# A rank count over a sparse adjacency: the last quarter of the rows moves from TensorE's recurrence to VectorE's scans

## The chip, the cores and the metric

One core of a Trainium2 chip runs the whole program. The metric is the device time of one execution in microseconds; three runs of the kernel before gave a median of 110.85 us (110.51 to 111.42).

## The reference, cut to what matters

The input is x (2048 x 64, f32) and a 0/1 adjacency adj (2048 x 2048, f32, about two ones in a row). Two graph layers follow each other, each with a residual and a layer norm:

```
support = x @ weight
rank = cumsum(adj != 0, axis=1); deg = rank[:, -1:]; k = min(deg, 100)
pos = rank - (deg - k)
w = mask * where(pos > 0, 0.5 ** (k - pos), 0)          # 2048 x 2048
x = layernorm(x + w @ support + bias)
deg = clip(sum(adj, 1) + 1, 1)
h = (adj @ x + x) / deg
z = concat([x, h]) @ W + b
x = layernorm(x + relu(z) / max(norm(relu(z)), 1e-12))
```

So in layer 0 every nonzero of a row gets a weight of one half to the power of the number of nonzeros to its right (beyond 100 it is zero). Layer 1 multiplies by the adjacency itself.

## The kernel before, in words

The rows are taken in four quarters q of 512, each as four tiles of 128 rows. The columns are taken in 16 blocks b of 128, from the right.

SyncE loads adj in 16 units of 1 MB (a quarter's 512 rows by 512 columns) into the ring `stage` of eight places; a place is loaded again when TensorE has transposed what lay there (lines 232 to 246). TensorE transposes two blocks of a unit at a time, 8 matmuls into one of two PSUM banks `tmp` (`transpose_adj`, line 834), and VectorE copies the bank to `adjT` (line 545). The last four of the 16 units, (2,1), (3,1), (2,0) and (3,0), go another way: VectorE casts them to `nat` (`pack`, line 497) and SyncE issues four DMA transposes (line 249).

The count is a recurrence in PSUM. `count` (line 856) adds block b with the triangular matrix `suffix` and block b+1 with `rest` to a bank `cnt` of 128 columns by 512 rows. ScalarE turns the bank into bf16 weights by a Relu that writes int16 (`weights`, line 326; the exponent bits are the count). The next `count` of the same bank waits until ScalarE has read it. `weigh` (line 870) multiplies the weights by `sup`, the support in three bf16 parts, in four matmuls of 192 columns, three steps behind. Two banks (c = 0 and 1) run next to each other: bank 0 takes quarter 0 and then quarter 2, bank 1 takes quarter 1 and then quarter 3, 16 steps each.

The order is written out by hand. TensorE's loop (line 970) runs over ticks: count of bank 0, weigh of bank 0, the transposition two ticks ahead (`fill`), count of bank 1, weigh of bank 1. VectorE and ScalarE have loops over the same marks (lines 506 and 348). Between the copies VectorE finishes quarters 0 and 1 (`finish_layer0`, line 458): part 0 sums the three parts out of PSUM, 1 adds x, 2 and 3 measure and centre, 4 is the inverse root and x1, 6 and 7 split y = x1 @ W for layer 1. `WHEN` says at which mark after a quarter's end each part stands, `X1T_AT` at which mark TensorE transposes x1.

After the ticks TensorE aggregates layer 1: `aggregate(g, blocks, tiles)` (line 903) is a row of 194-column matmuls from `adjT` and `ysp`. The parts that need only quarters 0 and 1 of y (`early`) cover VectorE's finish of quarters 2 and 3. GpSimd adds the identity to the diagonal blocks of `adjT` (line 285) before the aggregation reads them. VectorE, ScalarE and GpSimd then finish the output in five batches.

## Time and profile before

| | |
|---|---|
| median of three runs | 110.85 us |
| the profiled execution, its own time | 110.75 us |
| its span, first to last instruction | 108.8 us |
| TensorE matmul busy | 92.6 us, 85% |
| VectorE busy | 63.4 us, 58% |
| ScalarE busy | 57.4 us, 53% |
| GpSimd busy | 18.8 us, 17% |
| granted TensorE clock, mean | 0.974 |

The profiled execution took 1.95 us more than its span. Busy time is an average over stages; the stages here are the ticks (to about 75 us), the aggregation (to about 99 us) and VectorE's tail. Matmul durations are modelled and overlap; the distance between the starts of two matmuls says what one costs.

### The profile page before, as it was taken

The page shows a single profiled execution, that of the slowest core. Times are in us where ns is not written, and L with a number is a line of the kernel's source. Part 1 is how long each engine was busy: PE and PEld are TensorE (multiplying, and loading weights), DVE is VectorE, ACT ScalarE, POOL GpSimd, SP SyncE. Part 2 cuts the span into 40 slices and gives each one's busy share as a digit, 9 for nine tenths or more (in the row PEclk, how much of TensorE's full clock was granted, in tenths as well). Part 3 has the DMA queues.
Part 4 walks back from the last instruction along what each step waited for, and adds up shares of the span by engine and source line. Part 5 has one row for each costly group of instructions (what it writes and reads, how often), then busy time and mean ns, then how long its engine had stood idle before and what let it go on. Part 6 is the DMA issues. An engine that isn't in the chain of part 4 may idle for free.

```text
span 108.8 us, 2398 instructions
## 1 busy us (share of the span) xinstructions
PE 92.6 (85%) x886; PEld 72.4 (67%) x886; DVE 63.4 (58%) x188; ACT 57.4 (53%) x125; POOL 18.8 (17%) x44
## 2 busy tenths in 40 slices
PE   5938789999999999999996799999999999995000
PEld 2326448677778777776764477779989999994000
DVE  2224632352862424389799934148983339999991
ACT  0503866453766565756577486783032208478740
POOL 6200000000000009000009500000000000467860
PEclk9999999999999999999999999999999999999955
DMA  2999999999979999996979970000000000000124
GB/s 52 315 339 358 349 321 350 385 387 389 383 234 399 388 387 386 386 386 236 193 141 121 202 136 0 6 0 0 0 6 0 0 0 6 0 0 12 36 54 94
DMA packets 23867, 20.23 MB, mean 186 GB/s; under 512 B 13617, under 2 KB 17713, under 8 KB 23857
## 3 DMA queue, kind: packets, MB, share of 16 engines
q1 hardware_dynamic: 23696, 20.06, 60.4%
q8 instruction: 7, 0.11, 0.4%
q10 hardware_dynamic: 160, 0.03, 0.1%
q14 instruction: 4, 0.02, 0.1%
HBM read 17.47 MB, written 0.52 MB: 165 GB/s over the span
## 4 chain that ended last, share of the span: by engine, by line
PE 65%; DVE 17%; DMA 11%; issue 3%; ACT 1%; ACTq 1%; DVEq 0%
PE acc L878 17%; PE cnt L865 10%; PE cnt L867 10%; PE tmp L846 9%; PE acc L909 7%; DMA adjT<-nat 6%; DMA wd<-in_L_gnn_weight_dram 5%; PE cnt L909 5%; PE tmp L897 3%; DVE stats L447 3%; DVE t L582 3%; DVE adjT L545 2%; DVE t L593 1%; PE acc L923 1%; PE tmp L923 1%
## 5 line engine op out<-in xcount | busy, mean ns | idle before, releaser
L330 ACT ACTIVATE wts<-cnt 128x512 int16<-128x512 f32 x64 | 37.8, 596 | 20.4 <-PE cnt L867 20.1
L878 PEld LDWEIGHTS acc<-sup,wts 128*128 128x128 bf16 x256 | 22.8, 98 | 13.7 <-issue 0.5
L878 PE MATMUL acc<-sup,wts 128*128 128x192 bf16 x256 | 30.8, 246 | 0.0
L545 DVE COPY adjT<-tmp 128x1024 bf16<-128x1024 bf16 x24 | 16.4, 688 | 20.3 <-PE tmp L846 20.3
L865 PE MATMUL cnt<-adjT,rest 128*128 128x512 bf16 x60 | 22.7, 379 | 3.7 <-DMA adjT<-nat 1.6
L867 PE MATMUL cnt<-adjT,suffix 128*128 128x512 bf16 x64 | 24.2, 379 | 0.0
L285 POOL TENSOR_TENSOR adjT<-adjT,ident 128x128 bf16<-128x128 bf16 x16 | 7.3, 492 | 50.4 <-PE cnt L867 50.4
L846 PE MATMUL tmp<-ident,stage 128*128 128x128 bf16 x192 | 14.5, 219 | 0.7 <-DMA stage<-in_adj_dram 0.7
L846 PEld LDWEIGHTS tmp<-ident,stage 128*128 128x128 bf16 x192 | 12.3, 98 | 1.8 <-issue 1.2
L909 PE MATMUL acc<-ysp,adjT 128*128 128x194 bf16 x128 | 11.8, 247 | 0.0
L909 PEld LDWEIGHTS acc<-ysp,adjT 128*128 128x128 bf16 x128 | 10.8, 98 | 0.3
L289 POOL TENSOR_TENSOR small<-square,power 128x4 f32<-128x4 f32 (+1 forms) x4 | 4.2, 1053 | 33.4 <-DVE square L614 33.4
L865 PEld LDWEIGHTS cnt<-adjT,rest 128*128 128x128 bf16 x60 | 5.9, 98 | 5.6 <-ACT wts L330 3.0
L383 ACT ACTIVATE u<-u,degree 128x64 f32<-128x64 f32 x16 | 4.4, 336 | 4.8 <-DVE degree L578 4.7
L497 DVE CAST nat<-stage 128x512 bf16<-128x512 f32 x16 | 6.7, 467 | 0.1
L867 PEld LDWEIGHTS cnt<-adjT,suffix 128*128 128x128 bf16 x64 | 6.3, 98 | 0.3
L909 PE MATMUL cnt<-ysp,adjT 128*128 128x194 bf16 x64 | 6.0, 247 | 0.0
L447 DVE BATCH_NORM_STATS2 stats<-t 128x6 f32<-128x128 f32 x23 | 5.7, 285 | 0.1
L483 DVE TENSOR_TENSOR left<-tmp,ysp 128x256 f32<-128x256 f32 x4 | 1.7, 424 | 6.5 <-ACT ysp L341 6.5
L909 PE MATMUL tmp<-ysp,adjT 128*128 128x194 bf16 x64 | 5.5, 247 | 0.0
L909 PEld LDWEIGHTS cnt<-ysp,adjT 128*128 128x128 bf16 x64 | 5.4, 98 | 0.0
L909 PEld LDWEIGHTS tmp<-ysp,adjT 128*128 128x128 bf16 x64 | 5.3, 98 | 0.0
(101 smaller groups left out, 85.3 us busy)
## 6 DMA issues: line engine op xcount, KB each, us to landing
stage<-in_adj_dram SPq DMA_DIRECT2D x12, 1024.0 KB, 13.3
stage<-in_adj_dram SPq DMA_DIRECT2D x8, 512.0 KB, 8.0
xs<-in_x_dram SPq DMA_DIRECT2D x2, 256.0 KB, 6.0
out_dram<-xs SPq DMA_DIRECT2D x3, 128.0 KB, 2.0
out_dram<-xs SPq DMA_DIRECT2D x2, 64.0 KB, 1.7
wd<-in_L_gnn_W_dram SPq DMA_DIRECT2D x4, 16.0 KB, 7.9
adjT<-nat SPq DMA_TRANSPOSE x4, 5.0
wd<-in_L_gnn_weight_dram ACTq DMA_DIRECT2D x2, 16.0 KB, 4.8
```

Of the source, the lines that this page charges most:

```text
L285: nc.gpsimd.tensor_tensor(d, d, ident16[:, :], ALU.add).then_inc(diag_ready, 1)
L289: nc.gpsimd.tensor_tensor(small[:, 3, batch(k)], square[:, batch(k)], power[:, 0:size(k)], ALU.pow).then_inc(norm_ready[k], 1)
L330: nc.scalar.activation(wts[:, c, n % WRING, :].bitcast(I16), cnt[:, c, :], ACT.Relu).then_inc(w_ready[c], 1)
L383: nc.scalar.activation(u1[:, t, :], u1[:, t, :], ACT.Copy, scale=degree[:, t:t + 1]).then_inc(weighted[k], 1)
L447: yield nc.vector.bn_stats(stats[:, k, t:t + 2, :].rearrange("p s c -> p (s c)"), data[:, t:t + 2, :].rearrange("p t d -> p d t"))
L497: nc.vector.tensor_copy(nat[:, i, r, :], stage[:, u % RING, r, :]).then_inc(nat_ready, 1)
L545: nc.vector.tensor_copy(adjT[:, q, bp // 2, :, bp % 2 * 2:bp % 2 * 2 + 2, :], bank.bitcast(BF16).rearrange("p (r k n) -> p r k n", r=RT, k ...
L846: last = nc.tensor.transpose(bank[:, (2 * r + k) * P:(2 * r + k + 1) * P], halves[:, r, 2 * j0 + 1:2 * (j0 + P):2], ident16[:, :])
L865: nc.tensor.matmul(cnt[:, c, :], rest[:, :], block_of(q, b + 1), start=False, stop=False, skip_group_check=True)
L867: nc.tensor.matmul(cnt[:, c, :], suffix[:, :], block_of(q, b), start=(b == NB - 1), stop=True, skip_group_check=True).then_inc(cnt_done[c], 1)
L878: last = nc.tensor.matmul(acc[:, c * RT + r, 0:PD], wts[:, c, n % WRING, r * P:(r + 1) * P], sup[:, b, :], start=(b == NB - 1 and r % 2 == ...
L909: last = nc.tensor.matmul(agg[g][:, r, 0:PD + 2], adjT[:, g, b // QB, r, b % QB, :], ysp[:, b, 0:PD + 2], start=first, stop=(b == NB - 1), ...
```

## The change

Quarter 3 leaves the recurrence. Its rows are loaded as four tiles of 128 whole rows (1 MB each, the same ring). VectorE runs `tensor_tensor_scan` over each tile from the right, 512 columns at a time, 16 scans in all, at marks 11 to 27; each writes int16 ranks into the low halves of the f32 words it read. GpSimd turns the words into bf16 (`bare`, 16 times 128x512), SyncE transposes each tile by DMA (`turn`, 128x2048), ScalarE makes weights (`mix`, 16 times 128x512) and GpSimd makes 0/1 of the transposed tile again (`bare_adj`, four times 128x2048). TensorE weighs a tile by 16 matmuls (`weigh_tile`), the first three tiles in halves at the end of ticks 22 to 29, the fourth behind the loop. Bank 0's recurrence of quarter 2 runs alone in ticks 16 to 31.

All of quarter 2 is now transposed by TensorE (24 groups of 8 as before). The order of a tick is count, fill, weigh. The first count and the second transposition stand ahead of the support product. Quarters 0 and 1 are finished at earlier marks, two tiles of `aggregate(1, early)` run in ticks 30 and 31, and the addition of the bias to x goes from VectorE to GpSimd.

```diff
-TURNED = 4
-PARAMS_AT = 9
+PARAMS_AT = 11
...
-PIECES = {20: ((0, 0), (0, 1)), 21: ((0, 2), (0, 3)), 22: ((1, 0), (1, 1)), 23: ((1, 2), (1, 3)),
-          24: ((2, 0), (2, 1), (2, 2), (2, 3)), 25: ((3, 0), (3, 1)), 26: ((3, 2), (3, 3))}
-WHEN = {0: (0,), 5: (1, 2), 6: (3,), 7: (4,), 10: (6,), 11: (7,)}
-X1T_AT = 9
+SCANS = {11: (0, 3), 12: (0, 2), 13: (0, 1), 14: (0, 0), 15: (1, 3), 16: (1, 2), 17: (1, 1), 18: (1, 0),
+         19: (2, 3), 20: (2, 2), 21: (2, 1), 22: (2, 0), 24: (3, 3), 25: (3, 2), 26: (3, 1), 27: (3, 0)}
+SPREAD = {20: (0, 0), 21: (0, 2), 23: (1, 0), 24: (1, 2), 27: (2, 0), 28: (2, 2)}
+MIXES = {22: (0, 0), 23: (0, 2), 25: (1, 0), 26: (1, 2), 28: (2, 0), 29: (2, 2)}
+SOONER = {30: 2, 31: 3}
+UNITS = ((0, 3), (1, 3), (0, 2), (1, 2), (0, 1), (1, 1), (3, 0), (0, 0), (1, 0), (3, 1), (2, 3), (2, 2), (3, 2), (2, 1),
+         (3, 3), (2, 0))
+TURN_AT = {13: 0, 15: 1}
+WHEN = {0: (0,), 3: (1, 2, 3), 5: (4,), 7: (6,), 8: (7,)}
+X1T_AT = 6
...
 STEPS = 2 * NB
-TICKS = STEPS + BEHIND
+TICKS = STEPS
...
-        nat = sb("nat", [P, TURNED, RT, QB * P], BF16)
+        nat = sb("nat", [P, 2, N], BF16)
+        wts3 = sb("wts3", [P, 2, N], BF16)
+        minus = sb("minus", [P, 1], F32)
...
-            return (2 * (k // (NB // 2)) + c, NB // 2 - 1 - k % (NB // 2)) if 0 <= k < NB else None
-
-        units = sorted(((4 * j + BEHIND * c, 2 * (j // QB) + c, QB - 1 - j % QB) for j in range(2 * QB) for c in range(2)))
-        units = [(q, k) for _, q, k in units]
-
-        by_dma = units[len(units) - TURNED:]
+            return (2 * (k // (NB // 2)) + c, NB // 2 - 1 - k % (NB // 2)) if 0 <= k < (NB, NB // 2)[c] else None
+
+        units = list(UNITS)
...
+        rows_v = adj.rearrange("(q r p) n -> q r p n", r=RT, p=P)
+        turned3 = adjT[:, 3, :, :, :, :].rearrange("p a b c n -> p (a b c n)").rearrange("p (r b n) -> p r b n", r=RT, n=P)
+
+        def whole(u):
...
+            def turn(r):
+                sp.wait_ge(nat_ready, RT * (r + 1))
+                sp.dma_start_transpose(out=turned3[:, r, :, :], in_=nat[:, r % 2, :]).then_inc(turned[r], 16)
...
+                if u in TURN_AT:
+                    turn(TURN_AT[u])
                 if u >= RING:
                     oq, ok = units[u - RING]
-                    sp.wait_ge(tmp_full, number[("adj", oq, 2 * ok)] + 1)
-                sp.dma_start(stage[:, u % RING, :, :], adj_v[q, k]).then_inc(adj_loaded[u % RING], 16)
-            for i, (q, k) in enumerate(by_dma):
-                sp.wait_ge(nat_ready, RT * (i + 1))
-                sp.dma_start_transpose(out=adjT[:, q, k, :, :, :].rearrange("p r b n -> p (r b) n"),
-                                       in_=nat[:, i, :, :].rearrange("p r n -> p (r n)")).then_inc(turned[i], 16)
+                    if oq == 3:
+                        sp.wait_ge(nat_ready, RT * (ok + 1))
+                    else:
+                        sp.wait_ge(tmp_full, number[("adj", oq, 2 * ok)] + 1)
+                if q == 3:
+                    sp.dma_start(whole(u), rows_v[q, k]).then_inc(adj_loaded[u % RING], 16)
+                else:
+                    sp.dma_start(stage[:, u % RING, :, :], adj_v[q, k]).then_inc(adj_loaded[u % RING], 16)
+            turn(2)
+            turn(3)
...
+            def bare(r, h):
+                pool.wait_ge(ranked, RT * r + RT - h)
+                if r >= 2 and h == RT - 1:
+                    pool.wait_ge(turned[r - 2], 16)
+                n = slice(h * CH, (h + 1) * CH)
+                nc.gpsimd.tensor_scalar(nat[:, r % 2, n], whole(units.index((3, r)))[:, n], UNIT, -(UNIT + N), ALU.mult,
+                                        ALU.add).then_inc(nat_ready, 1)
+
+            def add_diagonal(q):
+                if q < 3:
+                    pool.wait_ge(cnt_done[q % 2], min(step(q, RT * q) + 2, (q // 2 + 1) * NB))
                 for b in range(RT * q, RT * q + RT):
-                    d = adjT[:, q, b // QB, b % RT, b % QB, :]
+                    if q == 3:
+                        pool.wait_ge(adj3_ready, b % RT + 1)
+                    d = adj_block(q, b, b % RT)
                     nc.gpsimd.tensor_tensor(d, d, ident16[:, :], ALU.add).then_inc(diag_ready, 1)
+
+            def bare_adj(r):
+                pool.wait_ge(w3_ready, RT * (r + 1))
+                nc.gpsimd.tensor_scalar(turned3[:, r, :, :], turned3[:, r, :, :], -2.0 * N, None,
+                                        ALU.is_gt).then_inc(adj3_ready, 1)
+
+            def tile(r):
+                for h in range(RT - 1, -1, -1):
+                    bare(r, h)
+
+            tile(0)
+            tile(1)
+            pool.wait_ge(par_loaded, 16 * 6)
+            pool.wait_ge(x_loaded[0], 16)
+            pool.wait_ge(x_loaded[1], 16)
+            pool.wait_ge(xT_done, 1)
+            pool.wait_ge(tmp_full, number[("xT", 0)] + 1)
+            nc.gpsimd.tensor_tensor(xs[:, :, :], xs[:, :, :], b0row[:, :].unsqueeze(1).to_broadcast([P, NB, D]),
+                                    ALU.add).then_inc(biased, 1)
+            add_diagonal(0)
+            add_diagonal(1)
+            tile(2)
+            bare_adj(0)
+            tile(3)
+            bare_adj(1)
+            add_diagonal(2)
+            bare_adj(2)
+            bare_adj(3)
+            add_diagonal(3)
...
+            def mix(r, h):
+                if h == 0:
+                    act.wait_ge(turned[r], 16)
+                if h == 0 and r >= 2:
+                    act.wait_ge(w3_used, r - 1)
+                nc.scalar.activation(wts3[:, r % 2, h * CH:(h + 1) * CH].bitcast(I16),
+                                     turned3[:, r, h * RT:(h + 1) * RT, :].rearrange("p b n -> p (b n)"), ACT.Relu,
+                                     scale=float(EXP1)).then_inc(w3_ready, 1)
...
-                    if tick == ENDS[q] + 5:
+                    if tick == ENDS[q] + 2:
...
-                if BEHIND <= tick < TICKS:
+                if BEHIND <= tick < NB + BEHIND:
                     weights(1, tick - BEHIND)
+                if tick in SPREAD:
+                    r, h = SPREAD[tick]
+                    mix(r, h)
+                    mix(r, h + 1)
+            for h in range(RT):
+                mix(3, h)
...
-                    dve.wait_ge(w_used[c], (q // 2 + 1) * NB)
+                    if q == 3:
+                        dve.wait_ge(w3_used, RT)
+                    else:
+                        dve.wait_ge(w_used[c], (q // 2 + 1) * NB)
...
+                    dve.wait_ge(biased, 1)
...
-            def pack(i, r):
-                u = len(units) - TURNED + i
-                if r == 0:
+            def scan(r, h):
+                u = units.index((3, r))
+                if h == RT - 1:
                     wait_adj(dve, u)
-                nc.vector.tensor_copy(nat[:, i, r, :], stage[:, u % RING, r, :]).then_inc(nat_ready, 1)
+                first, last = h * CH, (h + 1) * CH
+                low = whole(u).bitcast(I16)[:, 0:2 * N:2]
+                nc.vector.tensor_tensor_scan(out=low[:, first:last][:, ::-1], data0=whole(u)[:, first:last][:, ::-1],
+                                             data1=minus[:, 0:1].to_broadcast([P, CH]),
+                                             initial=float(TOP) if h == RT - 1 else low[:, last:last + 1],
+                                             op0=ALU.subtract, op1=ALU.mult).then_inc(ranked, 1)
...
-                if m == ENDS[0] + 4:
-                    dve.wait_ge(par_loaded, 16 * 6)
-                    dve.wait_ge(x_loaded[0], 16)
-                    dve.wait_ge(x_loaded[1], 16)
-                    link(nc.vector.tensor_tensor(xs[:, :, :], xs[:, :, :],
-                                                 b0row[:, :].unsqueeze(1).to_broadcast([P, NB, D]), ALU.add))
...
-                if group_at(m) and not turned_by_dma(m):
+                if group_at(m):
...
-                for i, r in PIECES.get(m, ()):
-                    pack(i, r)
+                if m in SCANS:
+                    r, h = SCANS[m]
+                    if h == RT - 1:
+                        dve.wait_ge(scan_set, 1)
+                    else:
+                        dve.wait_ge(ranked, RT * r + RT - 1 - h)
+                    scan(r, h)
...
-                if (q, b // QB) in by_dma:
-                    pe.wait_ge(turned[by_dma.index((q, b // QB))], 16)
-                else:
-                    read(("adj", q, b // 2))
+                read(("adj", q, b // 2))
...
+            def weigh_tile(r, blocks=range(NB)):
+                pe.wait_ge(acc_read, 2)
+                pe.wait_ge(w3_ready, RT * r + blocks[-1] // QB + 1)
+                for b in blocks:
+                    last = nc.tensor.matmul(acc[:, RT + r, 0:PD], wts3[:, r % 2, b * P:(b + 1) * P], sup[:, b, :],
+                                            start=(b == 0 and r % 2 == 0), stop=(b == NB - 1), skip_group_check=True)
+                if b == NB - 1:
+                    last.then_inc(w3_used, 1)
...
             transpose_adj(0)
+            pe.wait_ge(consts, 6)
+            count(0, 0)
+            transpose_adj(1)
             pe.wait_ge(w0_loaded, 32)
             pe.wait_ge(xT_ready, 1)
             support(1, acc_bank(6)).then_inc(sup_done, 1)
-            pe.wait_ge(consts, 6)
...
-                if group_at(m) and not turned_by_dma(m):
+                if group_at(m):
...
-            filled = 1
+            filled = 2
             for tick in range(TICKS):
-                if tick < STEPS:
+                if tick > 0:
                     count(0, tick)
-                if LAG <= tick:
-                    weigh(0, tick - LAG)
                 while filled <= tick + (1 if tick + 1 < FOLLOW else LEAD):
                     fill(filled)
                     filled += 1
-                if tick == TICKS - 1:
-                    for n in range(TICKS - LAG, STEPS):
-                        weigh(0, n)
-                if tick >= BEHIND:
+                if LAG <= tick:
+                    weigh(0, tick - LAG)
+                if BEHIND <= tick < NB + BEHIND:
                     count(1, tick - BEHIND)
-                if tick >= BEHIND + LAG:
+                if BEHIND + LAG <= tick < NB + BEHIND + LAG:
                     weigh(1, tick - BEHIND - LAG)
+                if tick in MIXES:
+                    r, h = MIXES[tick]
+                    weigh_tile(r, range(h * RT, (h + 2) * RT))
+                if tick in SOONER:
+                    pe.wait_ge(y_ready, 2)
+                    pe.wait_ge(diag_ready, PT)
+                    pe.wait_ge(w_ready[1], NB)
+                    aggregate(1, early, [SOONER[tick]])
             while filled < MARKS:
                 fill(filled)
                 filled += 1
-            for n in range(STEPS - LAG, STEPS - 1):
-                weigh(1, n)
+            for n in range(STEPS - LAG, STEPS):
+                weigh(0, n)
             pe.wait_ge(y_ready, 2)
-            pe.wait_ge(diag_ready, NB)
-            aggregate(1, early, [0])
-            weigh(1, STEPS - 1)
-            aggregate(1, early, [1, 2, 3])
+            pe.wait_ge(diag_ready, PT)
+            aggregate(1, early, [0, 1])
+            weigh_tile(3)
             pe.wait_ge(acc_read, 3)
             aggregate(0, early, [0])
...
             pe.wait_ge(acc_read, 4)
+            pe.wait_ge(diag_ready, PT + RT)
...
+            pe.wait_ge(diag_ready, NB)
```

## Rows read from the trace of the kernel before

**Rows 1.** The page: busy time, share of the span and instructions of each engine.

```profile
PE 92.6 (85%) x886; PEld 72.4 (67%) x886; DVE 63.4 (58%) x188; ACT 57.4 (53%) x125; POOL 18.8 (17%) x44
```

**Rows 2.** Busy time of the engines by stage, columns as its first row says.

```profile
core 0: us, PE busy (x) PEld busy (x) DVE busy (x) ACT busy (x) POOL busy (x), PEclk, DMA share, GB/s
...
42.00:60.50 18.50, 16.95 (x161) 12.25 (x159) 14.62 (x31) 11.86 (x21) 5.04 (x12) 1.00 0.99 253
60.50:75.20 14.70, 14.65 (x118) 10.97 (x119) 7.17 (x23) 10.17 (x21) 0.89 (x2) 1.00 0.28 56
```

**Rows 3.** Groups by line: ScalarE's weights, the count, VectorE's copy.

```profile
L330 ACT ACTIVATE wts<-cnt 128x512 int16<-128x512 f32 x64 | 37.8, 596 | 20.4 <-PE cnt L867 20.1
...
L867 PE MATMUL cnt<-adjT,suffix 128*128 128x512 bf16 x64 | 24.2, 379 | 0.0
...
L545 DVE COPY adjT<-tmp 128x1024 bf16<-128x1024 bf16 x24 | 16.4, 688 | 20.3 <-PE tmp L846 20.3
```

**Rows 4.** The timeline, one step of one bank and the next start.

```profile
61.52 0.38 PE L867 MATMUL cnt<-adjT,suffix 128*128 128x512 bf16 x1
61.74 0.49 PE L878 MATMUL acc<-sup,wts 128*128 128x192 bf16 x4
61.94 0.60 ACT L330 ACTIVATE wts<-cnt 128x512 int16<-128x512 f32 x1 [0.17 <-PE cnt L867]
...
62.07 0.38 PE L865 MATMUL cnt<-adjT,rest 128*128 128x512 bf16 x1
```

**Rows 5.** The timeline, the support product, and the first count of tick 16.

```profile
7.86 1.16 PE L923 MATMUL acc<-wd,t 128*128 128x128 f32 x8 [0.94 <-DMA wd<-in_L_gnn_weight_dram]
...
41.91 0.38 PE L867 MATMUL cnt<-adjT,suffix 128*128 128x512 bf16 x1
```

**Rows 6.** Groups: VectorE's f32 rows of 512 and 1024 columns.

```profile
L537 DVE TENSOR_TENSOR xs<-xs,b0row 128x1024 f32<-128x1024 f32 x1 | 1.2, 1217 | 0.0
...
L527 DVE TENSOR_TENSOR left<-sup 128x512 f32<-128x512 f32 x1 | 0.7, 691 | 0.1
```

**Rows 7.** The timeline, VectorE alone and while GpSimd ran.

```profile
53.51 0.75 DVE L497 CAST nat<-stage 128x512 bf16<-128x512 f32 x2
...
57.19 4.20 POOL L285 TENSOR_TENSOR adjT<-adjT,ident 128x128 bf16<-128x128 bf16 x8 [13.46 <-PE cnt L867]
...
57.64 1.21 DVE L497 CAST nat<-stage 128x512 bf16<-128x512 f32 x2
...
58.77 0.64 DVE L473 SCALAR_TENSOR_TENSOR t<-stats,t 128x256 f32<-128x256 f32 x1
```

**Rows 8.** The chain of waits: start, us, what; x1T(2), then aggregate(0, third).

```profile
78.91 0.22 PE tmp L888 x2
...
85.32 1.33 PE acc L909 x16
```

**Rows 9.** The timeline, quarter 3 summed and quarter 2 normed.

```profile
76.35 0.96 DVE L464 TENSOR_REDUCE t<-acc 128x256 f32<-128x768 f32 x1
77.22 0.17 DVE L452 RECIPROCAL small<-root 128x4 f32<-128x4 f32 x1
...
78.01 0.42 DVE L478 TENSOR_TENSOR x<-t,small 128x256 f32<-128x256 f32 x1
```

**Rows 10.** GpSimd's rows of 128 columns, and the DMA transposes.

```profile
L285 POOL TENSOR_TENSOR adjT<-adjT,ident 128x128 bf16<-128x128 bf16 x16 | 7.3, 492 | 50.4 <-PE cnt L867 50.4
...
L264 POOL TENSOR_SCALAR_AFFINE_SELECT ident<-ident 128x128 f32<-128x128 f32 x1 | 0.3, 292 | 0.2 <-POOL rest L261 0.2
...
DMA to landing us min/median/max: 4.3/5.0/6.1
```

**Rows 11.** Who waited for the DMA transposes.

```profile
PE cnt L865 <- DMA adjT<-nat: 1.6, 1, 1.6
```

**Rows 12.** TensorE and its clock after its last matmul.

```profile
99.00:100.00 1.00, 0.32 (x4) 0.09 (x2) 1.00 (x5) 0.90 (x5) 0.94 (x1) 1.00 0.00 0
...
103.00:104.00 1.00, 0.00 (x0) 0.00 (x0) 0.88 (x8) 0.63 (x2) 0.92 (x2) 0.55 0.48 111
```

## What the change does to the time, predicted before it was measured

> **What bounds the kernel now.** The page says TensorE: its matmuls are busy for 92.6 of 108.8 us, VectorE for 63.4 [rows 1]. That is an average, so the next view is the busy time by stage. In the second half of the ticks, 42 to 75 us, TensorE is busy for 16.95 of 18.5 us and then 14.65 of 14.7; VectorE has 14.62 of 18.5 us in the first of these stretches and half of the second [rows 2]. The only wait of size is one of 1.6 us on a DMA transpose [rows 11]. So two recurrences side by side leave TensorE no gap, and ScalarE's weights and the hand-over between engines are hidden: each bank's latency is covered by the other's work.
>
> The timeline of one step gives the prices. A matmul of 512 columns starts 0.22 us after the one before (the group's 379 ns is a modelled end [rows 3]), four weighing matmuls take 0.33 us, ScalarE starts 0.42 us after the second count matmul did and takes 0.60 us [rows 4, 3]. A lone bank can thus step no faster than 0.22 + 0.42 + 0.60 + 0.05 = 1.29 us, the 0.05 an estimate of the way back.
>
> **Part by part.** Removed: quarter 3's 31 count matmuls, 31 x 0.217 = 6.7 us of TensorE, the wait of 1.6 us, 16 of ScalarE's 0.60 us steps, VectorE's 16 casts (0.75 us for two [rows 7]) and its bias addition, 1.22 us [rows 6]. Weighing quarter 3 costs TensorE 64 matmuls as before, and the 24 groups of transpositions stay. Were TensorE's work all, the time would fall by 8.3 us to 102.4.
>
> Added to VectorE: 16 scans of 512 columns. No row shows a scan. From below the price is that of an elementwise row with as many elements, 0.69 us; from above by two such rows, one for each of its two operations, 1.38 us; between them lies the row of 1024 columns, 1.22 us [rows 6]. I take the 1.22 us: each element needs the finished result of its neighbour through two chained operations, subtract and multiply, which I charge as two passes over 512. With its wait on the scan before it I count 1.26 us. The Trainium skill says (DVE: opcode table, instruction layouts, handler registers and perf-mode slots, section Datapath and trigger behaviour) that the built-in scan program "runs at half throughput"; by that the price would be 0.69 us plus 512 cycles, an estimate of the same 1.22 us, and at one element a cycle it would be the 0.69 us of the rival below.
>
> **The ledger**, against the profiled execution (110.75 us, span 108.8; it stands 0.1 us below the median).
>
> (a) To tick 16. Before, quarter 2's first count starts at 41.91 us [rows 5]. In ticks 9 to 15 VectorE gets a copy (0.62 us between starts, 0.69 shown [rows 3]) and a scan per tick, 1.88 us, in a tick that takes 1.97 us: it keeps up by a hair. The support product (1.16 us [rows 5]) no longer stands before the first count; I give that 0.7 us, between none and all of it. One group of transpositions fewer falls into tick 15, 0.45 us. Tick 16 starts at 40.8 us.
>
> (b) Ticks 16 to 26. Here ticks could shrink to 1.3 to 1.9 us, but VectorE cannot follow. From 41.8 us (the copy of mark 18) to x1 of quarter 1 (mark 27) it has in its queue: 5 copies, 3.1 us; 8 scans, 10.1; two sums out of PSUM, 0.87 to 0.96 each by the tail's rows, 1.8; two times parts 1 to 3, 1.41 each, 2.8; two times part 4, from the reciprocal to the end of x1, 1.17 each, 2.3 [rows 9]. Sum 20.1 us; with small gaps x1 of quarter 1 is there at 62.1 us. TensorE needs three things from that queue. The count of tick 22 needs the copy of mark 22, which stands behind two scans and a sum: about 2 us of idling. The transposition of x1 of quarter 0 stands in tick 24, one mark ahead of the part of VectorE that makes it, and behind it the whole recurrence: 3.4 us. That of quarter 1 costs 0.6 us, and the bank for block pair 28 another 0.5.
>
> (c) From x1 of quarter 1 to layer 1. TensorE: the rest of tick 26, 2.3 us; tick 27 with its product of x1, 1.65; ticks 28 and 29 held by ScalarE, where two pieces of quarter 3's weights (0.60 each, as its other 512-column passes) stand between two steps of the chain, 2.15 and 2.2; tick 30, 1.45; then the last count, four weighings of 0.33, three tiles of aggregation at 0.67 and the fourth tile's weighing, 1.32: 5.05 us. Sum 14.8, so `aggregate(0)` starts at 76.9 us.
>
> (d) A new wait. VectorE's queue has quarter 3's sum ahead of quarter 2's inverse root. The sum now waits for `weigh_tile(3)`, which ends at 76.9 us, and TensorE has one tile (0.67 us) before it wants x1 of quarter 2. Latency 0.2, sum 0.9, root and x1 1.17 [rows 9]: x1 is transposed at 79.25 us, after 1.65 us of idling. Before, this stood at 78.91 us [rows 8]. From here to `aggregate(0, third)`, 6.4 us later [rows 8], and to the end the work is the same; quarter 3's y has as much cover as before relative to this mark.
>
> So far the change costs 0.35 us. The 8.3 us are used up by VectorE's backlog.
>
> (e) GpSimd beside VectorE. While GpSimd ran 4.20 us of additions, VectorE's casts took 1.21 us for two where 0.75 is normal, and a centring took 0.64 us [rows 7] where it takes 0.42 alone. In all 3.6 us of such instructions there had cost 2.3 us: 0.30 us are lost per us of GpSimd. In (b) GpSimd has the bias (about 2 us), 8 diagonal blocks (0.39 us between starts, 0.49 as shown [rows 10]), 8 `bare` and one `bare_adj`. A `bare` is bounded by the one-input row of 128 columns taken at 0.7 ns a column more, 0.56 us, and by the two-input row likewise, 1.1 us [rows 10]; I take the first, since it has one input. Together 11 us, of which two thirds lie under scans and other SBUF arithmetic: 7.2 x 0.30 = 2.2 us at most, nothing at least. By my price a scan asks for an element in every second cycle only, so I take half, 1.1 us.
>
> Hidden, with their cover: the DMA transposes land 4.3 to 6.1 us after issue [rows 10]; the first is wanted six ticks later, the fourth by ScalarE behind the loop, some 5 us after that. Without that cover each would cost its 5 us. SyncE's queue holds the loads of its last three units behind two of these issues, which wait for GpSimd; the last unit is then issued at about 48 us and wanted at 61. `bare_adj(3)` and the last diagonal blocks end near 79 us and are wanted at 91.
>
> Sum: 110.75 + 0.35 + 1.1 = 112.2 us.
>
> **Rivals.**
>
> *VectorE keeps up* (not slower). The scan costs 0.69 us, or little more. Then the queue in (b) is 4.2 us shorter and the lone bank and ScalarE bound the ticks; (d) stays. Of the 4.2 us some 3 reach the end and (e) shrinks: 110.75 + 0.35 - 3.0 = 108.1 us, and 107 if the wait for x1 in tick 24 goes as well. The point that decides is a scan of about 1.0 us. For it: VectorE has idle time in most ticks before [rows 2]. Against: the chained element. Chance 0.32.
>
> *GpSimd and the scans shut each other out* (slower still). If a scan holds the second operand's port for all of its 1.22 us, GpSimd's 7 us and the scans follow each other instead of overlapping; VectorE loses some 5 us, the end comes at 115.5 to 117. For it: rows 7. Against: both sides went on there, each at about two thirds. The skill (Advanced Engine Details and Errata, VectorE Performance Modes) says that GpSimd and two-port VectorE instructions "will interfere/block eachother"; the rows show interference, no block. Chance 0.11.
>
> *The clock falls.* It stayed at 1.00 for more than 3 us after the last matmul at 99.3 us and was 0.55 in the stretch from 103 [rows 12], on its way to the 1.2 GHz level. The idling in tick 24 is 3.4 us by (b), close to that. A few us of matmuls at half speed behind it cost 2 to 3 us: 114.5 us. Chance 0.08.
>
> The forecast case has 0.49, with a range of its own of 110.3 to 114.2 from (a)'s 0.7, (e)'s 2.2 and scans of up to 1.38 us (0.16 more each, of which 9 stand in (b)).
>
> **How the numbers follow.** A measurement of this kernel can tell about 1%, 1.1 us, from no change. The forecast case lies about evenly on both sides of 111.95: 0.25 slower, 0.22 same, 0.02 faster. The first rival gives 0.25 faster and 0.07 same, the other two 0.19 slower. Together: faster 0.27, same 0.29, slower 0.44. The range from 107.3 to 115.3 leaves out the shut-out port, most of what lies under 107.3, and no more.
>
> **What would show it.** In the trace after: the scan's duration, 1.22 us, decides first; VectorE without a gap from about 41 to 62 us; TensorE waiting for VectorE's copy in tick 22 and for x1 in tick 24; one wait of 1.6 us on x1 of quarter 2 near 78 us; VectorE's casts and centrings longer beside GpSimd; the granted clock at 1.00 to the end of aggregation. If the scan is under 1 us, or the ticks from 16 run at 1.3 to 1.9 us without waits, the forecast is wrong and the first rival holds. If TensorE waits on `turned` or on loads of `stage`, both are wrong.

## The result: slower by a tenth, and the profile after

The changed kernel takes 122.56 us (median of 4, 121.53 to 124.04) against 110.94 us (median of 4) of the kernel before beside it: a ratio of 1.104, with a 95% interval of 1.099 to 1.109. That is 11.6 us more, where 112.2 us, some 1.4 more, was forecast and 115.3 us was the top of the range. The direction was right, the size was not. Some executions of a kernel take a per cent or two more at a lower granted clock; the ratios and their intervals leave these out, the medians do not.

The page of the changed kernel, its engines (busy us, share of the span, instructions) and their share in 40 slices of 3.0 us:

```profile
span 120.7 us, 2347 instructions
...
PE 93.6 (78%) x855; PEld 74.4 (62%) x855; DVE 83.7 (69%) x188; ACT 56.2 (47%) x125; POOL 58.6 (49%) x65
...
PE   5957999898899998669209998996079999999000
...
DVE  2235633468799989999998956049985043999991
...
POOL 6200000000422569999996269999990000075870
PEclk9999999999999999976995999999955999999955
```

Against [rows 1], TensorE has two holes, each with one slice wholly empty, the 21st and the 29th (the digits 0), and a lower clock right behind each. GpSimd, off the path before, is busy for most of the time from 42 to 91 us. VectorE is at 9 tenths in the first hole. Who made TensorE wait (three of the entries; in us in total, times and longest):

```profile
PE tmp L985 <- DVE x L564: 10.1, 2, 5.3
PE cnt L953 <- DVE adjT L631: 2.9, 2, 2.3
PE tmp L937 <- DMA stage<-in_adj_dram: 1.7, 4, 0.6
```

The DMA transpose of [rows 11] is gone from this list. L985 transposes x1, and it waits twice for VectorE: 5.34 us for quarter 0 and 4.79 for quarter 2. So the next view is VectorE's timeline ahead of those two moments (start, duration, instruction), with GpSimd's and TensorE's beside it. Ahead of the first hole:

```profile
52.20 1.47 DVE L585 TENSOR_TENSOR_SCAN stage<-stage,minus 128x512 int16<-128x512 f32 x1
53.59 0.58 DVE L553 TENSOR_TENSOR t<-t,xs 128x256 f32<-128x256 f32 x1
...
54.73 0.58 DVE L559 SCALAR_TENSOR_TENSOR t<-stats,t 128x256 f32<-128x256 f32 x1
...
58.68 3.22 DVE L559 SCALAR_TENSOR_TENSOR t<-stats,t 128x256 f32<-128x256 f32 x1
...
62.74 0.42 DVE L564 TENSOR_TENSOR x<-t,small 128x256 f32<-128x256 f32 x1
```
```profile
54.42 3.43 POOL L312 TENSOR_SCALAR nat<-stage 128x512 bf16<-128x512 f32 x4
57.93 5.42 POOL L326 TENSOR_SCALAR adjT<-adjT 128x2048 bf16<-128x2048 bf16 x1
```
```profile
63.31 0.66 PE L985 MATMUL tmp<-ident,x 128*128 128x128 f32 x2 [5.34 <-DVE x L564]
```

A centring that takes 0.42 us alone takes 3.22, and it lies wholly inside one GpSimd instruction of 5.42 us: `bare_adj`, the comparison over 128x2048. The second hole has the same shape, with an instruction on 4 elements a partition in the victim's place:

```profile
83.94 0.17 DVE L534 RECIPROCAL small<-root 128x4 f32<-128x4 f32 x1
84.14 3.08 DVE L535 SCALAR_TENSOR_TENSOR small<-small 128x4 f32<-128x4 f32 x1
87.25 0.16 DVE L536 SCALAR_TENSOR_TENSOR small<-stats,small 128x4 f32<-128x4 f32 x1
```
```profile
78.13 10.80 POOL L326 TENSOR_SCALAR adjT<-adjT 128x2048 bf16<-128x2048 bf16 x2
```
```profile
88.22 0.66 PE L985 MATMUL tmp<-ident,x 128*128 128x128 f32 x2 [4.79 <-DVE x L564]
```

Two comparisons fill 78.13 to 88.93, 5.4 us each, so the second one starts near 83.5; the instruction of 0.16 us starts 0.6 us into it and ends 3.1 us later. The first of the two held something as well, late and so for a short time: an addition that takes 0.51 us in `e1_no_pass` starts 3.0 us into it and takes 0.91.

```profile
81.14 0.91 DVE L553 TENSOR_TENSOR t<-t,xs 128x256 f32<-128x256 f32 x1
```

The two groups (busy us, mean ns, idle before):

```profile
L585 DVE TENSOR_TENSOR_SCAN stage<-stage,minus 128x512 int16<-128x512 f32 x16 | 21.5, 1345 | 0.5 <-DMA stage<-in_adj_dram 0.4
L326 POOL TENSOR_SCALAR adjT<-adjT 128x2048 bf16<-128x2048 bf16 x4 | 21.5, 5376 | 0.3
```

The scan is what it was taken for: its shortest is 1.217 us. The four comparisons cost as much time as all sixteen scans, and the prediction had no price of its own for one. Last, TensorE by stage (stretch, length, busy and count, granted clock, share of DMA, GB/s):

```profile
54.00:58.00 4.00, 3.96 (x27) 0.69 1.00 298
58.00:62.00 4.00, 0.00 (x0) 1.00 0.73 145
62.00:64.00 2.00, 0.69 (x5) 0.82 0.00 0
64.00:66.00 2.00, 2.00 (x14) 0.50 0.04 8
66.00:68.00 2.00, 2.00 (x14) 0.82 0.00 0
84.00:86.00 2.00, 0.00 (x0) 1.00 0.00 0
86.00:88.00 2.00, 0.00 (x0) 0.80 0.00 0
88.00:90.00 2.00, 1.78 (x11) 0.50 0.00 0
90.00:93.00 3.00, 3.00 (x14) 0.50 0.00 0
93.00:97.00 4.00, 4.00 (x39) 0.87 0.00 0
```

TensorE works from 64 to 66 us and from 88 to 93 us at the lower level, 0.50 or 1.2 GHz, right behind its two holes. The four us before the first hole, 54 to 58, are at 0.69, with the wait of 2.27 us on the copy of mark 22 ahead of them. That wait need not bring the clock down: `e1_no_pass` has the same 2.27 us there and runs at 1.00 from 52 to 56 us.

### The profile page after: what moved, and what is told of

It is laid out like the page before. It is cut to its first block, busy times and chain, and to the rows that moved or that the text cites. A ratio compares the mean times of both kernels' runs of the same rounds, so it can differ in the third digit from the quotient of the medians.

```text
span 120.7 us, 2347 instructions
## 1 busy us (share of the span) xinstructions
PE 93.6 (78%) x855; PEld 74.4 (62%) x855; DVE 83.7 (69%) x188; ACT 56.2 (47%) x125; POOL 58.6 (49%) x65
## 4 chain that ended last, share of the span: by engine, by line
DVE 33%; PE 29%; DMA 28%; issue 5%; ACT 2%; SPq 1%; DVEq 0%
DMA stage<-in_adj_dram 28%; PE acc L1006 7%; DVE stage L585 6%; PE tmp L994 4%; DVE stats L529 4%; DVE t L559 4%; PE acc L966 3%; PE cnt L1006 3%; PE tmp L937 3%; DVE small L535 3%; DVE t L549 2%; DVE t L673 2%; PE cnt L953 2%; DVE adjT L631 2%; PE cnt L955 2%
## 5 line engine op out<-in xcount | busy, mean ns | idle before, releaser
L402 ACT ACTIVATE wts<-cnt 128x512 int16<-128x512 f32 x48 | 28.3, 596 | 26.1 <-PE cnt L955 26.0
L312 POOL TENSOR_SCALAR nat<-stage 128x512 bf16<-128x512 f32 x16 | 13.0, 820 | 39.6 <-DVE stage L585 39.5
L585 DVE TENSOR_TENSOR_SCAN stage<-stage,minus 128x512 int16<-128x512 f32 x16 | 21.5, 1345 | 0.5 <-DMA stage<-in_adj_dram 0.4
L326 POOL TENSOR_SCALAR adjT<-adjT 128x2048 bf16<-128x2048 bf16 x4 | 21.5, 5376 | 0.3
L966 PEld LDWEIGHTS acc<-sup,wts 128*128 128x128 bf16 x192 | 16.9, 101 | 6.7 <-issue 1.9
L953 PE MATMUL cnt<-adjT,rest 128*128 128x512 bf16 x45 | 17.6, 391 | 3.0 <-DVE adjT L631 2.9
L955 PE MATMUL cnt<-adjT,suffix 128*128 128x512 bf16 x48 | 18.7, 389 | 0.9 <-DVE adjT L631 0.9
L985 PE MATMUL tmp<-ident,x 128*128 128x128 f32 x8 | 2.1, 352 | 10.1 <-DVE x L564 10.1
L322 POOL TENSOR_TENSOR adjT<-adjT,ident 128x128 bf16<-128x128 bf16 x16 | 9.5, 622 | 0.2
L389 ACT ACTIVATE wts<-adjT 128x512 int16<-128x512 bf16 x16 | 9.0, 623 | 0.0
L985 PEld LDWEIGHTS tmp<-ident,x 128*128 128x128 f32 x8 | 1.1, 173 | 11.0 <-issue 10.8
L975 PE MATMUL acc<-sup,wts 128*128 128x192 bf16 x64 | 7.1, 261 | 0.3 <-ACT wts L389 0.2
L549 DVE TENSOR_REDUCE t<-acc 128x256 f32<-128x768 f32 x4 | 3.8, 943 | 4.6 <-PE acc L966 4.6
```

The source lines that it names most:

```text
L312: nc.gpsimd.tensor_scalar(nat[:, r % 2, n], whole(units.index((3, r)))[:, n], UNIT, -(UNIT + N), ALU.mult, ALU.add).then_inc(nat_ready, 1)
L322: nc.gpsimd.tensor_tensor(d, d, ident16[:, :], ALU.add).then_inc(diag_ready, 1)
L326: nc.gpsimd.tensor_scalar(turned3[:, r, :, :], turned3[:, r, :, :], -2.0 * N, None, ALU.is_gt).then_inc(adj3_ready, 1)
L389: nc.scalar.activation(wts3[:, r % 2, h * CH:(h + 1) * CH].bitcast(I16), turned3[:, r, h * RT:(h + 1) * RT, :].rearrange("p b n -> p (b n) ...
L402: nc.scalar.activation(wts[:, c, n % WRING, :].bitcast(I16), cnt[:, c, :], ACT.Relu).then_inc(w_ready[c], 1)
L585: nc.vector.tensor_tensor_scan(out=low[:, first:last][:, ::-1], data0=whole(u)[:, first:last][:, ::-1], data1=minus[:, 0:1].to_broadcast([ ...
```

## The experiments

**Theory A**: a long GpSimd comparison holds one VectorE instruction for some 3 us; two of these lie on the path, each opens a hole in TensorE's work, and the clock falls behind it. **Rivals**: (B) VectorE's queue is too long with the scans in it, whatever GpSimd does; (C) the lower clock is the main cost, whatever made the holes; (D) GpSimd delivers the weights too late.

**The operations by themselves** (`m1_beside`). A kernel that runs each pair alone and then together:

```
# (VectorE kind, VectorE count, GpSimd kind, GpSimd count), cut
("stt", 14, "gt", 1), ("tiny", 30, "gt", 1), ("scan", 5, "gt", 1), ("bank", 14, "gt", 1), ("cast", 14, "gt", 1),
...
if j == "gt":
    ins = nc.gpsimd.tensor_scalar(wide[:, a % 2, :], wide[:, a % 2, :], -4096.0, None, ALU.is_gt)
```

> A kernel of its own that computes nothing of the reference: it only stores x again, and runs VectorE and GpSimd instructions of this case first alone and then beside each other, phase by phase. Theory A (GpSimd's pass over 128x2048 bf16 holds VectorE's instructions that read two SBUF operands): alone the centring on 128x256 takes 0.42 us, the small one 0.16, the scan 1.22 to 1.28; beside one pass of 5.4 us (compare, bf16) at least one centring and at least one small instruction stand for 2 to 3 us, while subtractions from PSUM keep their 0.42 us. Theory B (the port is only shared): every two-operand instruction beside GpSimd takes 1.2 to 1.6 times its time alone and none stands for over 1 us. Open, both: whether the 5.4 us of the pass are the comparison's (a multiplication of the same size would take 1.7 to 2 us) or the size's.

This kernel ran once. Alone the comparison takes 5.36 us, a multiplication over the same row 5.36 as well. Beside it, VectorE's instructions, each line from its own stretch (minimum, median and maximum in ns): centrings of 256 columns (L102), tiny ones of 4 (L107), scans (L110), and subtractions with one operand in PSUM (L114).

```profile
L102 DVE SCALAR_TENSOR_TENSOR res<-stat,left x14: 409/411/3855, 42.0 to 49.9; 128x256 f32<-128x256 f32 x14
L107 DVE SCALAR_TENSOR_TENSOR little<-stat x30: 147/149/3615, 50.3 to 55.9; 128x4 f32<-128x4 f32 x30
L110 DVE TENSOR_TENSOR_SCAN ranks<-src,minus x5: 1193/1194/4586, 56.1 to 64.0; 128x512 int16<-128x512 f32 x5
L114 DVE TENSOR_TENSOR res<-acc,left x14: 414/414/424, 65.2 to 69.5; 128x256 f32<-128x256 f32 x14
```

Median and maximum say it: of each of the first three kinds one instruction is held, for 3.4 to 3.5 us over its own length, and the others run at full speed. Casts (0.42 us alone) had one of 5.58. The subtraction that reads PSUM is not held at all. Beside the shorter GpSimd work each instruction pays less: next to `bare`, a centring takes 0.82 and a scan 1.56 us; next to a diagonal block, 0.64 and 1.38. So A's account of the hold stands, and that of a port merely shared (none over 1 us) falls.

**Without the comparisons** (`e1_no_pass`):

```
-                nc.gpsimd.tensor_scalar(turned3[:, r, :, :], ..., ALU.is_gt).then_inc(adj3_ready, 1)
+                nc.gpsimd.memset(token[:, r:r + 1], 0.0).then_inc(adj3_ready, 1)
```

> The kernel after, but GpSimd's four passes over 128x2048 (bare_adj) are left out and a tiny memset stands in their place, so the last quarter's layer 1 sums are of ranks, not of ones. Theory A (the passes hold VectorE): the centring at 58.7 us goes from 3.2 to 0.4 to 0.6 us and the small instruction at 84.1 us from 3.1 to 0.16, TensorE's two waits for x1 shrink to 1.5 to 2.5 us each, the clock stays at 1.00, and the time falls from 122.6 to 113 to 115 us. Theory C (the miss is VectorE's backlog of scans and the order of its queue, the passes only ride along): the time stays above 118 us. Theory D (the clock): it matters only with a gap long enough, so as A, with TensorE at full clock as the larger part.

114.39 us, ratio 1.032 (1.026 to 1.038): 8.2 of the 11.6 us are the comparisons' doing. TensorE's waits in it:

```profile
PE tmp L985 <- DVE x L564: 5.4, 2, 3.7
PE cnt L953 <- DVE adjT L631: 3.2, 3, 2.3
```

3.75 us for quarter 0, 1.68 for quarter 2, and 2.27 for the copy of tick 22: this is the kernel that the prediction's (b) and (d) describe, with 3.4, 1.65 and "about 2". A goes through; 3.4 us remain for B and for the clock, for that falls here too, against what I expected, with the wait of 3.75 us (columns as above):

```profile
60.00:62.00 2.00, 1.92 (x14) 0.50 0.81 150
62.00:64.00 2.00, 2.00 (x7) 0.50 0.03 8
```

From the start of the transposition of x1 to that of the weighing L975, TensorE needs 4.90 us here (60.08 to 64.98) and 2.64 us for the same instructions at full clock (63.93 to 66.57 in `e3_keep_clock`). Some 2.3 of the 3.4 us may therefore be the clock's; no run has the comparisons left out and the clock kept up, so that split is an estimate.

**The comparisons cut into pieces** (`e8_pass_pieces`). All is computed, and GpSimd has the same columns to go through:

```
-                nc.gpsimd.tensor_scalar(turned3[:, r, :, :], turned3[:, r, :, :], -2.0 * N, None, ALU.is_gt)
+                for k in range(0, NB, 4):
+                    ins = nc.gpsimd.tensor_scalar(turned3[:, r, k:k + 4, :], turned3[:, r, k:k + 4, :], -2.0 * N, None, ALU.is_gt)
```

> The changed kernel, each of GpSimd's four comparing passes cut into four pieces of 128x512. Nothing else differs, and all is computed. If the time lost is in VectorE instructions that are held by one long GpSimd instruction (theory A), the 3.2 and 3.1 us ones shrink to 1 to 1.5 us each and the kernel comes to 118 to 120 us against 122.6. If what counts is how long GpSimd takes for the four passes (rival, 21.5 us before VectorE's and ScalarE's next users), the pieces sum to the same and the time stays at 122 to 124 us. If each piece holds VectorE as long as the whole (theory B), it is 124 to 128 us.

116.01 us, ratio 1.045 (1.041 to 1.050): 6.6 us back, more than I expected. Groups and instructions of this kernel (L327 is the comparison, L561 the centring, L537 the tiny one):

```profile
L327 POOL TENSOR_SCALAR adjT<-adjT 128x512 bf16<-128x512 bf16 x16 | 25.5, 1595 | 1.1
```
```profile
L561 DVE SCALAR_TENSOR_TENSOR t<-stats,t x4: 424/426/773, 56.4 to 84.3; 128x256 f32<-128x256 f32 x4
L537 DVE SCALAR_TENSOR_TENSOR small<-small x4: 164/205/319, 60.6 to 85.0; 128x4 f32<-128x4 f32 x4
```
```profile
61.79 0.41 PE L987 MATMUL tmp<-ident,x 128*128 128x128 f32 x2 [2.39 <-DVE x L566]
...
83.53 0.41 PE L987 MATMUL tmp<-ident,x 128*128 128x128 f32 x2 [1.75 <-DVE x L566]
```

GpSimd is busy for 4.0 us longer (25.5 against 21.5) and the kernel is 6.6 us faster. That rules out D and says where the loss sits: not in GpSimd's time but in single VectorE instructions held at a bad moment, with the waits and the clock that follow. The longest centring went from 3.22 to 0.77 us, the longest tiny one from 3.08 to 0.32.

**How the hold depends on the length** (`m2_hold`), with comparisons of 512, 1024 and 2048 columns, in place and into another buffer:

```
("stt", 12, "gt512", 4), ("stt", 10, "gt1024", 2), ("stt", 14, "gt2048", 1), ("stt", 12, "up512", 4), ("stt", 14, "copy", 1)
```

> A kernel of its own, which computes nothing of the reference: GpSimd compares bf16 rows with a constant over 128x512, 128x1024 and 128x2048 columns in place, over 128x512 and 128x2048 into another buffer, first alone, then with VectorE's STT over 128x256 (0.42 us alone) queued beside it. Theory A, GpSimd holds the shared path for a share of each instruction: alone 1.35, 2.7 and 5.36 us (2.6 ns a column), and one STT is held for about 0.9 us beside each 512-column piece, 1.8 beside 1024, 3.8 beside 2048, so that the sum held is the same however it is cut. Theory B, the hold is a fixed start-up cost of some 3.7 us: each 512-column piece holds one STT as long as the whole did. Theory C, it comes from reading and writing one and the same buffer: into another buffer no STT is over 0.9 us, and the piece itself is at the 0.6 us of the cast.

The centrings (L100) beside four pieces of 512, two of 1024, and one of 2048 into another buffer:

```profile
L100 DVE SCALAR_TENSOR_TENSOR res<-stat,left x12: 410/412/830, 34.2 to 39.2; 128x256 f32<-128x256 f32 x12
...
L100 DVE SCALAR_TENSOR_TENSOR res<-stat,left x10: 410/412/1257, 41.0 to 45.7; 128x256 f32<-128x256 f32 x10
...
L100 DVE SCALAR_TENSOR_TENSOR res<-stat,left x14: 410/412/3547, 62.6 to 70.1; 128x256 f32<-128x256 f32 x14
```

The longest was 0.83, 1.26 and (in place) 3.85 us: 0.4, 0.8 and 3.4 us over its own 0.41. So neither of my first two accounts fits: the hold isn't a fixed start-up, and it isn't a constant share of the columns either; it grows faster than the length. Another buffer changes little, 3.55 us, which ends the third account. Alone GpSimd takes 1.49, 2.77 and 5.36 us.

What fits is where the held centring ends. Here beside 1024 and beside 2048 columns:

```profile
41.09 3.00 POOL L81 TENSOR_SCALAR wide<-wide 128x1024 bf16<-128x1024 bf16 x1 [0.16 <-POOL wide L81]
41.38 1.26 DVE L100 SCALAR_TENSOR_TENSOR res<-stat,left 128x256 f32<-128x256 f32 x1
...
47.09 5.59 POOL L81 TENSOR_SCALAR wide<-wide 128x2048 bf16<-128x2048 bf16 x1 [0.15 <-POOL wide L81]
47.38 3.85 DVE L100 SCALAR_TENSOR_TENSOR res<-stat,left 128x256 f32<-128x256 f32 x1
```

It ends 1.45 us before GpSimd does in both (42.64 against 44.09, 51.23 against 52.68), and 0.60 us before it beside 512 columns. In the changed kernel the centring ends at 61.90, again 1.45 us before the comparison's 63.35, though it began 0.75 us into it; the tiny instruction ends 1.71 and the late addition (81.14) 1.44 us before. So a centring is held until the comparison is nearly through, however late it began. Two kinds don't fit into these numbers: the held scan of `m1_beside` ended 0.65 us before a comparison that itself took 6.33 us beside scans, and the held cast 0.28 us after its own. Why it is so is open.

**The comparisons on VectorE** (`e2_pass_on_dve`), three behind the last copy and the fourth behind quarter 2's y:

```
+            for r in range(3):
+                bare_adj(r)        # now nc.vector.tensor_scalar(turned3[:, r, :, :], ..., ALU.is_gt)
```

> The kernel after, with the four passes over 128x2048 moved from GpSimd to VectorE: three behind the last copy and the fourth behind quarter 2's y. Everything is computed. Theory A: VectorE takes 0.7 to 1.2 us for one (it was idle for 4.6 us before the sum of quarter 2), so the time is that without the passes plus 0 to 1 us: 113 to 116 us. Theory C: above 118 us.

114.22 us, ratio 1.022 (1.015 to 1.030). On VectorE such a comparison takes 0.68 to 0.92 us, against 5.36 on GpSimd. All is computed and it is no slower than leaving the comparisons out.

**The clock kept up** (`e3_keep_clock`): filler matmuls ahead of the two waits for x1, nothing else changed.

```
+            keep_warm(cnt[:, 1, :], 28)               # ahead of x1T(0)
+            keep_warm(tmp_bank(("x1T", 2)), 26)       # ahead of x1T(2)
```

> The kernel after, with 28 matmuls of 384 columns (4.5 us at full clock) on TensorE in front of the wait for x1 of quarter 0 and 26 in front of the one for x1 of quarter 2; their results are thrown away. Theory D (the clock's fall is a large part): the granted clock stays at 1.00 behind both waits, and the 3.5 us and 5 us that ran at 0.50 take half: 117.5 to 119.5 us. Theory A: the waits themselves stay (VectorE is as late as before), only the clock's part goes, 2 to 4 us of the 11.7.

119.90 us, ratio 1.083 (1.075 to 1.091): 2.7 us back, and the granted clock is 1.00 behind both waits. The centring is still at 3.22 us and the tiny one at 3.08. C is a quarter of the loss, and it follows from the holes.

**Quarter 2's chain ahead of quarter 3's sum** (`e4_tail_order`), on top of the version with the comparisons on VectorE (`e2_pass_on_dve`):

```
-            for q, part in (..., (2, 3), (3, 0), (2, 4), (3, 1), ...
+            for q, part in (..., (2, 3), (2, 4), (3, 0), (3, 1), ...
```

> The kernel with the passes on VectorE (114.2 us), and in VectorE's queue quarter 3's sum put behind quarter 2's inverse root and x1 instead of ahead of it. Step (d) of the prediction says that this order costs a wait of 1.65 us on x1 of quarter 2; in the run before it was 2 to 3 us. Theory A (order of the queue is part of what is left): that wait falls under 0.5 us and the time to 112 to 113 us. Theory E (TensorE would wait for quarter 3's x1 right behind it instead): no more than 0.5 us is gained.

112.92 us, 1.017 (1.009 to 1.024). The wait for x1 of quarter 2 falls from 1.68 to 0.53 us: the new wait of the prediction's (d) was real, and an accident of the order. What that is worth in time is not shown: the ratios differ by 0.6 us and their intervals overlap.

**x1 asked for one mark later** (`e5_x1_later`), on top of e4:

```
-WHEN = {..., 7: (6,), 8: (7,)}
-X1T_AT = 6
+WHEN = {..., 8: (6,), 9: (7,)}
+X1T_AT = 7
```

> The kernel before it in this list, and x1 of quarters 0 and 1 transposed by TensorE one mark later (X1T_AT = 7), with the parts of VectorE and ScalarE that follow it. Theory A (TensorE meets VectorE's backlog at the wait for x1 of quarter 0, one mark ahead of its maker): the wait of 3 us in tick 24 shrinks by a tick's 1 to 2 us and the time falls by 1 us or more. Theory C (VectorE's backlog is the bound whatever stands where): the wait moves to a copy and less than 0.5 us is gained.

112.03 us, 1.007 (1.003 to 1.012; 10 runs, one of which, at 237 us, stands apart unexplained). About 1 us came back, but not as I expected: the wait for x1 of quarter 0 went from 1.95 to 1.81 us only, where it was to shrink by 1 to 2 us. VectorE has that x1 ready at 61.4 instead of 60.7 us, and the profile shows it behind already ahead of these parts (the sum ends at 49.1 against 48.5).

**GpSimd's work away from the ticks** (`e6_pool_apart`), on top of e5: the bias addition at 23 us instead of 45, and the diagonal blocks of quarters 0 and 1 behind the last tile.

```
-            tile(0); tile(1); pool.wait_ge(par_loaded, 16 * 6)          # then the bias
-            add_diagonal(0); add_diagonal(1); tile(2); tile(3)
+            pool.wait_ge(b0_loaded, 16)                                 # then the bias
+            tile(0); tile(1); tile(2); tile(3); add_diagonal(0); add_diagonal(1)
```

> The kernel before it, and GpSimd's other two-operand work taken from beside the scans: the bias addition runs at about 22 us, before the first scan (its row is loaded from ScalarE's queue at the start), and the diagonal blocks of quarters 0 and 1 behind the fourth tile. Theory B (shared port, step (e)): the scans of marks 18 to 22 go from 1.4 to 1.6 us back to 1.28, VectorE's queue is 1 to 1.5 us shorter and so is the time: 110 to 111 us, no slower than the kernel before the change. Against it: under 0.4 us, if that time is waited out elsewhere.

110.29 us, 0.995 (0.992 to 0.998): 1.7 us back by the medians, 1.3 by the ratios. In the version it was made from, the scan of mark 19 ran beside the bias addition:

```profile
44.85 2.35 POOL L335 TENSOR_TENSOR xs<-xs,b0row 128x1024 f32<-128x1024 f32 x1
45.51 2.77 DVE L581 TENSOR_TENSOR_SCAN stage<-stage,minus 128x512 int16<-128x512 f32 x1 [1.32 <-DMA stage<-in_adj_dram]
```

It took 2.77 us, after 1.32 us of waiting for its load, and TensorE waited 2.77 us for the sum behind it. In `e6_pool_apart` this scan takes 1.19 us without a wait for the load, and TensorE waits 0.38. The later scan of mark 22 goes from 1.48 to 1.27. So a GpSimd instruction of 2.35 us can hold a scan too. The edit also moved the load of the bias row from SyncE's queue to ScalarE's, and the run doesn't separate the load that came in time from the addition that was gone.

**Half the scan** (`e7_half_scans`), on top of e6:

```
-                first, last = h * CH, (h + 1) * CH
+                first, last = h * CH + CH // 2, (h + 1) * CH
```

> The kernel before it with every scan over 256 columns instead of 512: half the ranks of the last quarter are left out, everything else runs. A scan takes 1.22 - 256 x 2 / 0.96 GHz = 0.69 us. Theory F (the scans' length is what is left of the loss: VectorE's queue bounds ticks 16 to 27): 9 scans in that stretch give back 4.8 us, of which 3 reach the end: 107 to 108.5 us. Theory G (the lone recurrence and ScalarE bound the ticks by now): less than 1 us.

108.10 us, 0.973 (0.969 to 0.978), within what was expected. A scan takes 0.69 us here. With GpSimd's longest work out of the way, half the scans' length was worth 2.2 us: that is what is left of rival B.

**The last scans a mark later** (`e9_scans_back`), on top of e6, all computed:

```
-... 22: (2, 0), 24: (3, 3), 25: (3, 2), 26: (3, 1), 27: (3, 0)}
+... 23: (2, 0), 25: (3, 3), 26: (3, 2), 27: (3, 1), 28: (3, 0)}
```

> The version with the passes on VectorE and GpSimd's other work apart (110.3 us), with the scans of marks 22 and 24 to 27 one mark later. All is computed. If the scans ahead of the copies of marks 22 and 24 are what makes TensorE wait (1.8 and 1.6 us), and the last rows' tile has slack, 108.5 to 109.5 us. If VectorE's queue is full whatever the order, what is won at mark 22 is lost at the end of the scans, whose last tile goes through the transposing DMA and ScalarE right before TensorE uses it (at 74.6 and 75.6 us in the version before): 110 to 111.5 us.

109.36 us, 0.988 (0.984 to 0.993): 1.2% faster than the kernel before, the version that computes everything and beats it by about what can be told. Its waits for x1 of quarters 0 and 2:

```profile
PE tmp L984 <- DVE x L554: 0.7, 2, 0.5
```

against 2.2 us in the version it was made from. The end of the scans had slack, then, which speaks against a queue that is full whatever its order.

## Why the prediction was wrong

**The step that failed is (e), GpSimd beside VectorE.** It counted "8 `bare` and one `bare_adj`" in (b), "Together 11 us", and gave the `bare_adj` no price of its own; beside the bias (2), eight diagonal blocks (3.1) and eight `bare` (4.5) the sum leaves it 1.4 us. It then charged 0.30 us per us of GpSimd, a rate taken from short additions [rows 7], and halved the result to 1.1 us. The comparison takes 5.36 us, and what it does to VectorE is no rate but one instruction held until the comparison is nearly through, here for 3 us. Twice that instruction was on the chain to x1. The row to price it from was there: one instruction has as many columns as four `bare`, and 128 columns take 0.49 us [rows 10], so that sixteen times that, 7.8 us, was an upper bound worth writing down. Measured: 8.2 us of the loss go when the comparisons are left out, 6.6 when they are only cut.

**The rival that came nearest was given 0.11.** "GpSimd and the scans shut each other out" had the right kind of event and the wrong victims, and its 115.5 to 117 us fall short by over 5 us. It was turned away with "the rows show interference, no block". The rows were of 128-column instructions. The Trainium skill's sentence (Advanced Engine Details and Errata, VectorE Performance Modes), that the two "will interfere/block eachother", was quoted, and the softer half taken. The runs show both: 0.2 to 0.4 us more beside short instructions, a block of over 3 us beside a long one. For the victim it names VectorE's two-port instructions. The cast held in `m1_beside` (5.58 us) agrees with that. A centring, a tiny instruction and a scan were held as well, which the table of that section doesn't list as two-port instructions, and subtractions with an operand in PSUM were not. The scans themselves were hardly the victims: at 1.345 us on average they cost 1.4 us in all over the 1.26 counted.

**"The clock falls" (0.08) was the second thing put at nothing.** The forecast case had a wait of 3.4 us in tick 24 and the clock at 1.00 behind it. In `e1_no_pass`, without a comparison, the wait is 3.75 us, the clock is 0.50 from 58 to 64 us, and the kernel takes 114.39 us, where this rival said 114.5. In the changed kernel the fall costs 2.7 us by `e3_keep_clock`, within its "2 to 3 us".

**The scan's price** was right: 1.217 us alone against 1.22 taken. By the Trainium skill (DVE: opcode table, instruction layouts, handler registers and perf-mode slots, section Datapath and trigger behaviour) it was to be 1.22 as well, at half throughput; the trace agrees. With it "VectorE keeps up" fell, as far as the scan goes.

**(a)** said tick 16 starts at 40.8 us. It starts at 41.66, 0.25 us before [rows 5] and not 1.1. The first count, now ahead of the support product, waits 0.88 us for its copy, and the support product starts at 8.59 us where it did at 7.86; and from 22 to 33 us TensorE waits 1.35 us for loads of adj, where it had no such wait. 0.9 us too little.

**(b)** had the waits in their places and about their sizes, as the version without comparisons shows: 3.75 us for x1 of quarter 0 (forecast 3.4), 2.27 for the copy of tick 22 (about 2). VectorE's queue from the copy of mark 18 to x1 of quarter 1 was to take 20.1 us. It took 23.0 without the comparisons (42.08 to 65.07 us) and 25.8 with them (42.52 to 68.30). Of the 2.9 us in between, 1.5 are scans lengthened by `bare`, bias and diagonals, 0.7 the lengthened parts 1 to 3, and the rest short waits and part 4; the last 2.8 us are the held centring, 3.22 less 0.42.

**(c)** was 14.8 us from x1 of quarter 1 to `aggregate(0)`. From 68.30 to 82.60 us it is 14.3.

**(d)** had the new wait at 1.65 us. Without comparisons it is 1.68; in the changed kernel 4.79, the held instruction being the tiny one of quarter 2's inverse root. From there to `aggregate(0, third)` it said 6.4 us, "the work is the same" [rows 8]. TensorE ran at half clock from 88 to 93 us, and it took 9.3 (88.22 to 97.55).

These steps add up. In trace time `aggregate(0, third)` was forecast at 85.7 us and starts at 97.55, 11.9 us later: 6.2 us by the end of (b), (a)'s 0.9 among them, 0.5 less in (c), 3.3 in (d) (5.62 us from `aggregate(0)` to the transposition, 2.35 forecast), and 2.9 behind it. Some 5.7 us of it are the two held instructions, counted over the 0.42 and 0.16 us that they take alone. The rest, for which no run has a split, is the clock, the longer scans and (a)'s 0.9 us.

Of the signs that were to show it, the gapless VectorE, the two waits in ticks 22 and 24 and the scan's duration came in. "The granted clock at 1.00 to the end of aggregation" didn't. The sign against it, a wait of TensorE on loads of `stage`, came in small: 1.7 us, against 0.7 before. The DMA transposes landed 4.3 to 10.2 us after issue, up to 4 us later than [rows 10], and TensorE waited for none of them.

## What to carry to other kernels

Price every instruction that is moved to GpSimd by its own columns and ask, for each one, which single VectorE instruction it could hold and whether that one is on the path: that one waits until GpSimd's is nearly through, so a long one blocks and a short one costs a few tenths of a us. If it must be there, cut it: 21.5 us of comparisons in four instructions cost 6.6 us more than 25.5 us in sixteen. And before moving work onto an engine with idle time, look where its queue's next hand-over stands: with the comparisons on VectorE, the order of the work and one load in another queue took the ratio from 1.022 to 0.988.

## What the runs showed of the hardware

- GpSimd needs 2.6 us per 1000 columns of bf16 into bf16 (5.36 us for 2048), in place or not, comparing or multiplying, but 0.62 us for 512 columns of f32 into bf16. 512 columns of bf16 into bf16 take 1.49 us, more than twice as long.
- Beside a GpSimd instruction of 2048 columns one VectorE instruction on SBUF is held, 3.85 us for one of 0.41 and 3.62 for one of 0.15; those behind it run at full speed while GpSimd goes on. A held centring ends 1.45 us before a comparison of 1024 or 2048 columns does, and 0.60 us before one of 512. The hold adds 0.4 us beside 512 columns and 0.8 beside 1024.
- A scan that started 0.66 us into a GpSimd addition of 2.35 us (two operands, 1024 columns of f32) took 2.77 us.
- A subtraction with one operand in PSUM isn't touched by it: 414 to 424 ns for all fourteen.
- A scan, 1.19 to 1.22 us alone, takes 1.56 beside `bare` and 1.38 beside a diagonal block.
